# u*B of 16 of the 64 tiles made with time on the partitions, in a 12-layer state-space kernel

## The chip, the cores and the metric

The kernel runs on one core of one Trainium2 chip. The metric is the device time in microseconds; three runs gave 21105.7 to 21121.04 us, median 21120.72.

## The reference

The input x has 8 images of 256 channels and 32x32 = 1024 points; the points are the time steps. Twelve layers follow each other. A layer does, for each image (einsums written short):

```
xn = layernorm(x); xp = xn @ proj_w + pb; z = silu(xp)
forward:  xs = softplus(xp @ convf_w + b);   backward: the same with convb_w, time reversed
delta, B, C = split(xs @ dbc_w)      # 32 ranks, 16 states of B, 16 states of C
delta = softplus(delta @ dtp_w + dtp_b)
h[t] = exp(delta[t]*A[n]) * h[t-1] + (delta[t]*xs[t]) * B[t,n]     # per channel and state n
y[t] = sum over n of h[t]*C[t,n];    y += xs*D
out = x + (y_forward + y_backward) * z
```

With u = delta*xs, the input of the scan of state n is u[channel, t] * B[t, n]. All data are float32.

## The kernel before

An image in a layer is one iteration; there are 12 x 8 = 96 of them. Channels stand on the 128 partitions (two channel halves), time runs along the free dimension (1024 columns). One iteration has 64 tiles: channel half (k // 32), direction ((k // 16) % 2), state (k % 16). In one tile:

- ScalarE makes dA = exp(delta * A[n]) (`tile_exp`, L507) into one of four buffers.
- TensorE replicates row n of B over all partitions into PSUM (`rep_b`, L666, two bf16 matmuls: B is held as three bf16 parts and `select` adds them), VectorE multiplies it by u in place (`times_b`, L802), and scans (`scan`, L818) into a ring of eight buffers.
- A DMA on SyncE loads row n of C, broadcast over the partitions (`load_c`, L285), GpSimd multiplies the scan by it (`product`, L356), and TensorE adds the result into y by a matmul with the identity (`add_up`, L676), five tiles later (LAG).

Eight of the 64 tiles (`SHARED`) do without TensorE and VectorE's multiply: SyncE loads the row of B from HBM (L291), GpSimd multiplies it by u into `v` (L364), and ScalarE puts exp into the PSUM buffer that B would have had.

Each engine has its own instruction list and goes through it in order. The list is written as slots, one per tile. VectorE takes two tiles at a time: multiply k, multiply k+1, scan k, scan k+1. TensorE's slot k is: `rep_b` of tile k+2 (it waits for scan k, which frees the PSUM buffer), the add-up of tile k-5, any `add_skip` (xs*D by a diagonal matrix, L687), then `prepare(k)`. `prepare` is the work for the next iteration (layernorm, projections, softplus, B and C, delta and u): tables such as `CONV_AT`, `DTP_AT` say in which slot each step stands, with first and second entries for the two directions, and for halves or channel groups. ScalarE's tables count three slots later (`AHEAD`): its `prepare(k)` comes after the exp of tile k+3. TensorE's preparation matmuls are L694 (over two channel halves, 4 instructions) and L741 (one matmul, 2 instructions), through two PSUM banks `bank[0]`, `bank[1]`, which ScalarE empties: `both_signs` (L511 Abs and L512 Relu) after projections and after L741. GpSimd's are the normalisation (L372), the sums of softplus (L391, L396), the split of B into bf16 parts (L381, L386) and u (L404). VectorE has the centring (L832) and the gate `finish` (L824), which waits for the last add-up of a channel half. The waits are semaphores: `h_ready` counts scans, `p_ready` products, `summed` add-ups, `b_ready` replications, `u_ready` u's, `dtp_out` emptied banks.

Of the kernel before, what the change touches and what calls it, by code (L numbers as in the profile page):

```python
# [17 lines left out]
def conv_seq_kernel(nc, x, ln_g, ln_b, proj_w, proj_b, convf_w, convf_b, convb_w, convb_b,  # L18
# [17 lines left out]
    NDA, NR, NC = 4, 8, 4  # L36
# [845 lines left out]
```

## Time and profile before

| | busy us | share of the span |
|---|---|---|
| VectorE (DVE) | 20038.9 | 95% |
| GpSimd (POOL) | 19962.6 | 95% |
| TensorE (PE) | 18408.8 | 87% |
| ScalarE (ACT) | 11624.8 | 55% |
| DMA read from HBM | 3744.62 MB | 184 GB/s over the span |
| span of the profiled execution | 21097.6 | |
| its own device time | 21099.31 | |
| median of the three runs | 21120.72 | |

The busy time of an engine is the time in which one of its instructions was running; two that overlap count once. A row of the timeline has the start, the length of a run of equal instructions, and in brackets the idle time before it and what ended it. The granted clock of TensorE was 0.979 of full speed on the average.

### The profile page before, as it was taken

To read this page: it belongs to the slowest core of one execution; us is meant where nothing else is said; L and a number is where in the kernel's file an instruction comes from. 1 tells how busy PE (TensorE), PEld (TensorE's weight loads), DVE (VectorE), ACT (ScalarE), POOL (GpSimd) and SP (SyncE) were. 2 spreads that over 40 slices of the span, in tenths; PEclk is the share of its full clock that TensorE was granted. 3 is DMA by queue.
4 is the path that set the end of the run, shared out by engine and by line. 5 is a ranking of instruction groups with operands and counts; after the bars stand their busy time and mean duration, and the time that the engine had idled before them with its cause. 6 is when DMAs were issued, how large, how long until landed. Compare 5 with 4: busy or idle time off the path is not lost.

```text
span 21097.6 us, 191673 instructions
## 1 busy us (share of the span) xinstructions
PE 18408.8 (87%) x45506; PEld 7540.0 (36%) x46368; DVE 20038.9 (95%) x11904; ACT 11624.8 (55%) x12409; POOL 19962.6 (95%) x8174
## 2 busy tenths in 40 slices
PE   8888888888888888888888888888888888888888
PEld 3333333333333333333333333333333333333333
DVE  7999999999999999999999999999999999999999
ACT  5555555555555555555555555555555555555554
POOL 8999999999999999999999999999999999999998
PEclk9999999999999999999999999999999999999999
DMA  5555555555555555555555555555555555555555
GB/s 170 184 186 185 187 179 190 183 184 186 181 186 186 183 187 183 188 181 186 185 186 186 181 189 183 185 186 182 187 184 182 187 184 188 181 186 186 184 186 175
DMA packets 1101818, 3886.20 MB, mean 184 GB/s; under 512 B 147584, under 2 KB 158336, under 8 KB 1100416
## 3 DMA queue, kind: packets, MB, share of 16 engines
q1 hardware_dynamic: 1023616, 3733.38, 50.5%
q0 software_dynamic: 26112, 100.67, 2.7%
q10 hardware_dynamic: 50688, 36.88, 0.7%
q8 instruction: 463, 7.59, 0.1%
q14 instruction: 939, 7.69, 0.1%
HBM read 3744.62 MB, written 134.22 MB: 184 GB/s over the span
## 4 chain that ended last, share of the span: by engine, by line
issue 34%; DVE 20%; PE 19%; POOL 17%; ACT 4%; DMA 4%; DVEq 1%; ACTq 1%; POOLq 0%; SPq 0%
DVE ring L818 13%; PE y L676 11%; POOL ring L356 10%; DVE bv L802 6%; DMA c<-c_rows 4%; PE bv L666 3%; PE bank L694 3%; POOL delta L396 3%; ACT dA L507 2%; POOL parts L386 1%; PE bank L741 1%; DVE w L832 1%; POOL u L404 1%; POOL v L364 1%; POOL dbc L381 1%
## 5 line engine op out<-in xcount | busy, mean ns | idle before, releaser
L356 POOL TENSOR_TENSOR ring<-ring,c 128x1024 f32<-128x1024 f32 x6144 | 14327.9, 2372 | 209.8 <-DVE ring L818 200.8
L676 PE MATMUL y<-ring,ident 128*128 128x512 f32 x24576 | 11798.1, 608 | 620.3 <-POOL ring L356 526.8
L818 DVE TENSOR_TENSOR_SCAN ring<-dA,bv 128x1024 f32<-128x1024 f32 x5376 | 12021.6, 2271 | 100.2
L507 ACT ACTIVATE dA<-delta,a_step 128x1024 f32<-128x1024 f32 x5376 | 6022.4, 1146 | 2834.1 <-DVE ring L818 2238.9
L802 DVE TENSOR_TENSOR bv<-u,bv 128x1024 f32<-128x1024 f32 x5376 | 6332.4, 1214 | 844.7 <-POOL u L404 416.8
L676 PEld LDWEIGHTS y<-ring,ident 128*128 128x128 f32 x24576 | 4759.9, 195 | 4967.1 <-issue 3536.8
L666 PE MATMUL bv<-parts,select 128*128 128x512 bf16 x9890 | 3111.5, 390 | 1915.7 <-DVE ring L818 1856.0
L666 PEld LDWEIGHTS bv<-parts,select 128*128 128x128 bf16 x10752 | 729.5, 99 | 5732.1 <-DVE ring L818 5122.7
L507 ACT ACTIVATE bv<-delta,a_step 128x1024 f32<-128x1024 f32 x768 | 859.5, 1119 | 2426.8 <-DVE ring L818 2289.4
L364 POOL TENSOR_TENSOR v<-u,v 128x1024 f32<-128x1024 f32 x768 | 1812.3, 2360 | 124.6 <-DMA v<-c_rows 123.3
L818 DVE TENSOR_TENSOR_SCAN ring<-bv,v 128x1024 f32<-128x1024 f32 x768 | 1739.3, 2265 | 24.3 <-ACT bv L507 24.1
L694 PE MATMUL bank<-z,wt 128*128 128x512 f32 x3072 | 1442.5, 592 | 0.8 <-ACT z L533 0.8
L511 ACT ACTIVATE tmp<-bank,vec 128x512 f32<-128x512 f32 x768 | 525.4, 684 | 1155.3 <-PE bank L694 927.4
L372 POOL TENSOR_TENSOR w<-w,tmp 128x1024 f32<-128x1024 f32 x192 | 453.9, 2364 | 725.5 <-ACT tmp L608 725.5
L511 ACT ACTIVATE pre<-bank,vec 128x512 f32<-128x512 f32 x768 | 527.5, 687 | 924.2 <-PE bank L694 571.8
L741 PE MATMUL bank<-dbc,wt_dbc 128*128 128x512 f32 x1536 | 777.4, 608 | 119.5 <-ACT delta L512 113.7
L694 PEld LDWEIGHTS bank<-z,wt 128*128 128x128 f32 x3072 | 583.5, 190 | 735.9 <-issue 731.9
L694 PE MATMUL bank<-pre,mean_w 128*128 128x512 f32 x1536 | 733.3, 600 | 6.5 <-DMA pre<-in_x_dram 5.8
L694 PE MATMUL bank<-w,wt 128*128 128x512 f32 x1536 | 692.8, 594 | 1.3 <-ACT wt L492 1.3
L527 ACT ACTIVATE pre<-w 128x1024 f32<-128x1024 f32 x192 | 202.9, 1057 | 772.0 <-DVE w L832 772.0
L559 ACT COPY dbc<-bank 128x512 f32<-128x512 f32 x384 | 220.3, 574 | 636.5 <-POOL parts L386 397.4
L533 ACT ACTIVATE z<-bank,pbias 128x512 f32<-128x512 f32 x384 | 251.6, 680 | 524.4 <-PE bank L694 524.4
(65 smaller groups left out, 10686.0 us busy)
## 6 DMA issues: line engine op xcount, KB each, us to landing
c<-c_rows SPq DMA_DIRECT2D x6144, 512.0 KB, 4.5
v<-c_rows SPq DMA_DIRECT2D x768, 512.0 KB, 5.0
out_dram<-z POOLq DMA_DIRECT2D x96, 1024.0 KB, 11.9
pre<-out_dram SPq DMA_DIRECT2D x88, 1024.0 KB, 5.2
c_rows<-dbc ACTq DMA_DIRECT2D x192, 128.0 KB, 1.9
pre<-in_x_dram SPq DMA_DIRECT2D x8, 1024.0 KB, 5.0
out_dram<-in_x_dram SPq DMA_DIRECT2D x8, 1024.0 KB, 15.9
raw_w<-in_L_conv_proj_w_dram ACTq DMA_DIRECT2D x12, 256.0 KB, 5.3
```

The lines of the kernel that those rows point to most:

```text
L356: nc.gpsimd.tensor_tensor(ring[k % NR][:], ring[k % NR][:], c_sb[k % NC][:], ALU.mult).then_inc(p_ready, 1)
L364: nc.gpsimd.tensor_tensor(v_sb[:], u_of(d, s)[:, c, :], v_sb[:], ALU.mult).then_inc(vp_ready, 1)
L372: nc.gpsimd.tensor_tensor(wh, wh, tmp[:, 0:1, half(h)].to_broadcast([P, DT, HALF]), ALU.mult).then_inc(normed, 1)
L396: nc.gpsimd.tensor_tensor(delta_of(d, s)[:], delta_of(d, s)[:], scratch[j][:], ALU.add).then_inc(delta_ready, 1)
L507: nc.scalar.activation(to[:], delta_of(d, s)[:, c, :], ACT.Exp, scale=a_step[s][:, c, n:n + 1]).then_inc(da_ready, 1)
L511: nc.scalar.activation(scratch[j][:, e, half(h)], bank[i % 2][:], ACT.Abs, bias=bias).then_inc(abs_done, 1)
L666: mm = pe.matmul(bv[k % 2][:, half(h)], select[:, n:n + 1].to_broadcast([P, P]), parts_of(d, s)[:, half(h)], start=True, stop=True)
L676: mm = pe.matmul(y[:, half(h)], ident[:], ring[k % NR][:, half(h)], start=(k % HALF_TILES == 0), stop=(k % HALF_TILES == HALF_TILES - 1), ...
L694: mm = pe.matmul(dst[:], lhs(c), rhs[:, c, half(h)], start=(c == 0), stop=(c == DT - 1))
L741: pe.matmul(bank[i % 2][:], wt_dbc[:, DT + e, :], dbc[:, half(h)], start=True, stop=True).then_inc(dtp_ready, 1)
L802: nc.vector.tensor_tensor(bv[k % 2][:], u_of(d, s)[:, c, :], bv[k % 2][:], ALU.mult).then_inc(v_ready, 1)
L818: nc.vector.tensor_tensor_scan(h, a, b, 0.0, ALU.mult, ALU.add).then_inc(h_ready, 1)
```

## The change

No tile is shared with GpSimd any more. For 16 tiles (`BY_T`: every odd tile from 17 to 31 and from 49 to 63) u*B is made as follows.

- B of the direction of these tiles is turned once per iteration: TensorE transposes the eight 128-column blocks of `dbc` (`turn_b`), ScalarE copies the 16 columns of each block out (`b_t`, time on the partitions).
- u of the channel half and direction of these tiles is turned twice per iteration, for tiles 16 to 31 and for 48 to 63: TensorE transposes eight blocks into the two banks (`turn_u`), ScalarE copies them to `u_t`. In the next slot with preparation work TensorE waits for these copies.
- For each of the 16 tiles ScalarE scales the eight blocks of `u_t` by the column of `b_t` (one value of B per time step, that is per partition) into `v_t` (`scale_u`), right after the exp of the tile before, and TensorE transposes the eight blocks back into the PSUM buffer `bv` (`turn_v`), where `rep_b` of the tile would stand. VectorE scans from there, with dA from SBUF.

The loads of B rows on SyncE and the products u*B on GpSimd are gone. There are three dA buffers instead of four (tile 63 takes the buffer of 61). HELD goes from 2 to -21. The tables of `prepare`, `SKIPS`, `LOADX_AT` (50 to 63) and `W_AT` are new. At the very end GpSimd's memset writes `mark`.

```diff
-    NDA, NR, NC = 4, 8, 4
-    SHARED = (9, 19, 23, 29, 35, 45, 55, 59)
-    B_AHEAD, V_AHEAD = 5, 6
-    LAG, HELD = 5, 2
+    NDA, NR, NC = 3, 8, 4
+    BY_T = (17, 19, 21, 23, 25, 27, 29, 31, 49, 51, 53, 55, 57, 59, 61, 63)
+    UT_GROUPS = (1, 3)
+    UT_AT, UT_OUT_AT = (1, 37), (1, 36)
+    BLOCKS = T // P
+    LAG, HELD = 5, -21
...
-    MEAN_AT, CENTRE_AT, SQUARE_AT = (3, 4), (8, 10), (7, 10)
-    VAR_AT, RSTD_AT, NORM_AT = (9, 11), (11, 15), (9, 16)
-    PROJ_AT, XP_AT = (15, 15, 19, 19), (16, 16, 19, 19)
-    CONV_AT = ((22, 23, 25, 27), (29, 31, 33, 35))
-    CONV_OUT_AT = ((21, 23, 28, 29), (29, 30, 33, 34))
-    XS_LOG_AT, XS_AT = ((31, 32), (35, 35)), (35, 39)
-    DBC_AT, DBC_OUT_AT = ((37, 39), (47, 49)), ((37, 39), (47, 48))
-    DTP_AT, DTP_OUT_AT = ((41, 41, 41, 42), (49, 51, 51, 51)), ((40, 41, 42, 42), (50, 50, 52, 52))
-    HI_AT, REST_AT, MID_AT, PARTS_AT = (40, 49), (44, 53), (45, 57), (47, 55)
-    DELTA_LOG_AT, DELTA_AT, U_AT = ((43, 47), (55, 55)), (47, 55), (47, 57)
-    DIAG_AT, A_STEP_AT = 49, 53
-    GATE_AT = 37
-    LOADX_AT = 50
-    W_AT = 55
-    SKIPS = ((13, 9), (51, 55))
+    MEAN_AT, CENTRE_AT, SQUARE_AT = (3, 7), (6, 9), (7, 9)
+    VAR_AT, RSTD_AT, NORM_AT = (9, 11), (11, 11), (10, 15)
+    PROJ_AT, XP_AT = (13, 17, 18, 18), (18, 18, 20, 21)
+    CONV_AT = ((23, 23, 26, 26), (31, 31, 33, 35))
+    CONV_OUT_AT = ((23, 23, 26, 29), (31, 32, 32, 35))
+    XS_LOG_AT, XS_AT = ((30, 31), (35, 36)), (36, 38)
+    DBC_AT, DBC_OUT_AT = ((37, 38), (43, 48)), ((37, 37), (46, 50))
+    BT_AT, BT_OUT_AT = 39, 38
+    DTP_AT, DTP_OUT_AT = ((39, 40, 40, 41), (50, 51, 51, 51)), ((40, 40, 40, 41), (50, 51, 52, 52))
+    HI_AT, REST_AT, MID_AT, PARTS_AT = (38, 50), (42, 55), (43, 55), (44, 56)
+    DELTA_LOG_AT, DELTA_AT, U_AT = ((42, 44), (52, 56)), (46, 56), (47, 57)
+    DIAG_AT, A_STEP_AT = 47, 31
+    GATE_AT = 40
+    LOADX_AT = 63
+    W_AT = 54
+    SKIPS = ((13, 9), (51, 56))
...
+        def da_of(k):
+            return k % NDA if k < TILES - 1 else (k - 2) % NDA
+        def da_gap(k):
+            return next(g for g in range(1, 2 * NDA) if da_of((k - g) % TILES) == da_of(k))
...
 # ScalarE
-                if k in SHARED:
-                    act.wait_ge(h_ready, tiles(it, k - 1))
-                    to = bv[k % 2]
-                else:
-                    act.wait_ge(h_ready, tiles(it, k + 1 - NDA))
-                    to = dA[k % NDA]
+                act.wait_ge(h_ready, tiles(it, k + 1 - da_gap(k)))
...
+            def turn_u(it, g):
+                for h in range(NH):
+                    act.wait_ge(ut_turned, uts(it, g) + (h + 1))
+                    act.wait_ge(vt_ready, others(it, g * NS))
+                    nc.scalar.copy(u_t[:, h * (BLOCKS // NH):(h + 1) * (BLOCKS // NH), :].rearrange("p b d -> p (b d)"),
+                                   bank[h][:]).then_inc(ut_out, 1)
+            def scale_u(it, k, s):
+                n, g = k % NS, k // NS
+                act.wait_ge(ut_out, uts(it, g) + NH)
+                act.wait_ge(bt_out, it * NH + NH)
+                act.wait_ge(v_turned, others(it, k))
+                for q in range(BLOCKS):
+                    one = nc.scalar.activation(v_t[:, q, :], u_t[:, q, :], ACT.Copy, scale=b_t[s][:, q, n:n + 1])
+                one.then_inc(vt_ready, 1)
...
 # TensorE
+            def turn_b(n, j):
+                pe.wait_ge(dbc_out, n * 4 + 2 * j + 2)
+                for q in range(BLOCKS):
+                    h, r = q // (BLOCKS // NH), q % (BLOCKS // NH)
+                    mm = pe.transpose(bank[h][:, r * P:(r + 1) * P], dbc[:, q * P:(q + 1) * P], ident[:])
+                mm.then_inc(bt_turned, 1)
...
+            def turn_v(it, k):
+                pe.wait_ge(vt_ready, others(it, k + 1))
+                pe.wait_ge(h_ready, tiles(it, k - 1))
+                for q in range(BLOCKS):
+                    mm = pe.transpose(bv[k % 2][:, q * P:(q + 1) * P], v_t[:, q, :], ident[:])
+                mm.then_inc(v_turned, 1)
...
                         if k == DTP_AT[j][i]:
+                            if j == 0 and i == 0:
+                                pe.wait_ge(bt_out, n * NH + NH)
...
-                    if (k + 2) % TILES in SHARED:
-                        pass
+                    if (k + 2) % TILES in BY_T:
+                        turn_v(it, k + 2)
...
+                    for g, at in zip(UT_GROUPS, UT_AT):
+                        if k == at:
+                            turn_u(it, g, at, s, more)
+                        if k == next(f for f in range(at, TILES) if f in fills) and more:
+                            pe.wait_ge(ut_out, uts(it, g) + NH)
...
 # VectorE
-                if k in SHARED:
-                    dve.wait_ge(vp_ready, others(it, k + 1))
-                    a, b = bv[k % 2][:], v_sb[:]
+                if k in BY_T:
+                    dve.wait_ge(v_turned, others(it, k + 1))
```

## Rows read from the trace of the kernel before

**Rows 1.** The page, part 1: busy us (share of the span) x instructions.
```profile
PE 18408.8 (87%) x45506; PEld 7540.0 (36%) x46368; DVE 20038.9 (95%) x11904; ACT 11624.8 (55%) x12409; POOL 19962.6 (95%) x8174
```

**Rows 2.** Groups of instructions by form: xcount | busy us, mean ns | idle before, releasers.
```profile
L356 POOL TENSOR_TENSOR ring<-ring,c 128x1024 f32<-128x1024 f32 x6144 | 14327.9, 2372 | 209.8 <-DVE ring L818 200.8 <-issue 4.7 <-DMA c<-c_rows 1.5
L818 DVE TENSOR_TENSOR_SCAN ring<-dA,bv 128x1024 f32<-128x1024 f32 x5376 | 12021.6, 2271 | 100.2
...
L802 DVE TENSOR_TENSOR bv<-u,bv 128x1024 f32<-128x1024 f32 x5376 | 6332.4, 1214 | 844.7 <-POOL u L404 416.8 <-PE bv L666 339.6 <-issue 88.2
...
L364 POOL TENSOR_TENSOR v<-u,v 128x1024 f32<-128x1024 f32 x768 | 1812.3, 2360 | 124.6 <-DMA v<-c_rows 123.3
```

**Rows 3.** Timeline of VectorE, a shared and an own pair: start us, us, instruction.
```profile
10001.73 1.21 DVE L802 TENSOR_TENSOR bv<-u,bv 128x1024 f32<-128x1024 f32 x1
10003.07 2.29 DVE L818 TENSOR_TENSOR_SCAN ring<-dA,bv 128x1024 f32<-128x1024 f32 x1
...
10007.45 2.33 DVE L802 TENSOR_TENSOR bv<-u,bv 128x1024 f32<-128x1024 f32 x2
10009.70 4.46 DVE L818 TENSOR_TENSOR_SCAN ring<-dA,bv 128x1024 f32<-128x1024 f32 x2
10014.07 1.21 DVE L802 TENSOR_TENSOR bv<-u,bv 128x1024 f32<-128x1024 f32 x1
```

**Rows 4.** The gate's line, 9900 to 10900 us: ns min/median/max, first and last start.
```profile
L824 DVE TENSOR_TENSOR z<-y,z x9: 1225/1225/1225, 9959.5 to 10836.3; 128x1024 f32<-128x1024 f32 x9
```

**Rows 5.** Waits over the span: us in total, times, longest us.
```profile
DVE bv L802 <- POOL u L404: 416.8, 96, 91.5
...
DVE bv L802 <- PE bv L666: 339.6, 274, 1.8
```

**Rows 6.** Timeline of GpSimd at the end of an iteration.
```profile
10151.58 4.50 POOL L404 TENSOR_TENSOR u<-delta,xf 128x2048 f32<-128x2048 f32 x1
```

**Rows 7.** The page, part 6: KB each, median us from issue to landing.
```profile
pre<-out_dram SPq DMA_DIRECT2D x88, 1024.0 KB, 5.2
```

**Rows 8.** Timeline of TensorE, slots of around tile 50.
```profile
10323.99 0.61 PE L666 MATMUL bv<-parts,select 128*128 128x512 bf16 x2
10324.44 1.88 PE L676 MATMUL y<-ring,ident 128*128 128x512 f32 x4
10326.15 1.88 PE L694 MATMUL bank<-xf,wt_dbc 128*128 128x512 f32 x4
10327.87 1.02 PE L741 MATMUL bank<-dbc,wt_dbc 128*128 128x512 f32 x2
```

**Rows 9.** Transposes of weights, timeline; then a stretch: us, busy, PEclk, DMA, GB/s.
```profile
19098.19 0.38 PE L644 MATMUL bank<-ident,raw_dbc 128*128 128x128 f32 x2
19098.41 0.38 PE L644 MATMUL bank<-ident,raw_dtp 128*128 128x128 f32 x2
19098.63 1.88 PE L676 MATMUL y<-ring,ident 128*128 128x512 f32 x4
...
19097.00:19100.00 3.00, 0.60 (x4) 0.50 (x4) 1.00 1.00 391
```

**Rows 10.** Timeline of ScalarE: column scalings, exp, Abs, Relu.
```profile
10330.54 0.69 ACT L599 ACTIVATE diag_d<-ident,vec 128x128 f32<-128x128 f32 x2
10331.13 1.14 ACT L507 ACTIVATE dA<-delta,a_step 128x1024 f32<-128x1024 f32 x1
10332.17 0.67 ACT L511 ACTIVATE tmp<-bank,vec 128x512 f32<-128x512 f32 x1
10332.74 0.68 ACT L512 ACTIVATE delta<-bank,vec 128x512 f32<-128x512 f32 x1
```

**Rows 11.** Timeline of VectorE: the multiply of tile 25 waits for TensorE.
```profile
10240.07 1.23 DVE L802 TENSOR_TENSOR bv<-u,bv 128x1024 f32<-128x1024 f32 x1 [1.26 <-PE bv L666]
```

**Rows 12.** TensorE's last L741 of slot 51, and VectorE behind it.
```profile
10337.21 1.10 PE L741 MATMUL bank<-dbc,wt_dbc 128*128 128x512 f32 x2 [0.59 <-ACT delta L512]
...
10338.77 1.23 DVE L802 TENSOR_TENSOR bv<-u,bv 128x1024 f32<-128x1024 f32 x1 [1.61 <-PE bv L666]
```

More of the change, by code:

```diff
@@ L123, in conv_seq_kernel @@
         c_sb = [sb(f"c{i}", [P, T]) for i in range(NC)]
-        v_sb = sb("v", [P, T])
+        u_t = sb("u_t", [P, BLOCKS, P])
+        v_t = sb("v_t", [P, BLOCKS, P])
+        b_t = [sb(f"b_t{s}", [P, BLOCKS, NS]) for s in range(2)]
         raw_w = sb("raw_w", [P, DT, D])
@@ L141, in conv_seq_kernel @@
         eps = sb("eps", [P, 1])
+        mark = sb("mark", [P, 1])
         c_rows = nc.dram_tensor("c_rows", (2, DIRS, BC, T), F32, kind="Internal").ap()
@@ L425, in tail @@
                 pool.wait_ge(gated, it * DT + DT)
-                nc.gpsimd.memset(v_sb[:, 0:1], 0.0)
+                nc.gpsimd.memset(mark[:], 0.0)
                 finish(it, s, b)
@@ L559, in prepare @@
                             nc.scalar.copy(dbc[:, half(h)], bank[h][:]).then_inc(dbc_out, 1)
+                    if j == 0 and k == BT_OUT_AT:
+                        act.wait_ge(bt_turned, n + 1)
+                        for h in range(NH):
+                            nc.scalar.copy(b_t[s][:, h * (BLOCKS // NH):(h + 1) * (BLOCKS // NH), :],
+                                           bank[h][:].rearrange("p (b r) -> p b r", r=P)[:, :, 0:NS]).then_inc(bt_out, 1)
                     for i, (e, h) in enumerate(layers_steps):
@@ L613, in slots @@
                     tile_exp(it, k, s)
+                    if k + 1 in BY_T:
+                        scale_u(it, k + 1, s)
+                    for g, at in zip(UT_GROUPS, UT_OUT_AT):
+                        if k - AHEAD == at:
+                            turn_u(it, g)
                     if more:
@@ L668, in rep_b, with banks_free, turn_u @@
                 mm.then_inc(b_ready, 1)
+            def turn_b(n, j):
[4 more added lines that the diff above has]
+                mm.then_inc(bt_turned, 1)
+            def banks_free(k, n):
+                if k <= MEAN_AT[0]:
+                    pe.wait_ge(dtp_out, n * (2 * FILLS))
+                elif PROJ_AT[-1] < k <= CONV_AT[0][0]:
+                    pe.wait_ge(xp_ready, n * FILLS + FILLS)
+                elif CONV_AT[0][-1] < k <= CONV_AT[1][0]:
+                    pe.wait_ge(conv_out, n * (2 * FILLS) + FILLS)
+                else:
+                    assert CONV_AT[1][-1] < k <= DBC_AT[0][0]
+                    pe.wait_ge(conv_out, n * (2 * FILLS) + 2 * FILLS)
+            def turn_u(it, g, at, s, more):
+                c, d = g // DIRS, g % DIRS
+                if g == UT_GROUPS[0]:
+                    pe.wait_ge(u_ready, it * 2 + 2)
+                else:
+                    pe.wait_ge(ut_out, uts(it, g))
+                if more:
+                    banks_free(at, it + 1)
+                for q in range(BLOCKS):
+                    h, r = q // (BLOCKS // NH), q % (BLOCKS // NH)
+                    mm = pe.transpose(bank[h][:, r * P:(r + 1) * P], u_of(d, s)[:, c, q * P:(q + 1) * P], ident[:])
+                    if r == BLOCKS // NH - 1:
+                        mm.then_inc(ut_turned, 1)
+            def turn_v(it, k):
+                pe.wait_ge(vt_ready, others(it, k + 1))
+                pe.wait_ge(h_ready, tiles(it, k - 1))
+                for q in range(BLOCKS):
+                    mm = pe.transpose(bv[k % 2][:, q * P:(q + 1) * P], v_t[:, q, :], ident[:])
+                mm.then_inc(v_turned, 1)
             def add_up(it, k):
@@ L838, in slots @@
                     times_b(it, k, s)
-                    if k + 1 not in SHARED:
+                    if k + 1 not in BY_T:
                         times_b(it, k + 1, s)
```

39 lines of the change are left out of this document (18 added, 21 removed).

## The prediction

> **What bounds the kernel now.** I read the busy shares first. VectorE and GpSimd are both busy 95% of the span, TensorE 87%, ScalarE 55% [rows 1]. The costliest groups say what the two do: for each of 6144 tiles GpSimd makes one product by C (2.33 us apart), and for 768 of them it also makes u*B (2.36 us); VectorE makes one scan per tile (2.2 us apart) and 5376 products u*B [rows 2]. The timeline of VectorE gives the true step costs. A pair of tiles that VectorE prepares itself takes 6.62 us (10007.45 to 10014.07). A pair with one shared tile takes 5.72 us (10001.73 to 10007.45): two back-to-back products cost 1.12 each, but a lone one costs 1.34, because the scan waits for its result [rows 3]. So a tile taken away from VectorE is worth 0.90 us, not the 1.21 of its product.
>
> The gate operations show the period: nine of them, two per iteration (one image through one layer), from 9959.5 to 10836.3, so 876.8/4 = 219.2 us [rows 4]. VectorE's work in it: 24 pairs x 6.62 + 8 x 5.72 = 204.6, and two gates and two centrings of 1.1 to 1.2 with 0.3 of wait at each gate, about 5.1 together: 209.7. The rest, 9.5 us, is waiting. The waits name it: 416.8 us for GpSimd's u (91.5 of it the prologue, so 3.4 per iteration) and 339.6 for TensorE's B (3.5 per iteration) [rows 5]. The first is GpSimd's own load: it starts the last u at 10151.58 and ends it after 10156.0, when the next iteration could have begun [rows 6].
>
> **What the change takes away.** Turned tiles go from 8 (shared) to 16. VectorE: eight more pairs become 5.72: -8 x 0.90 = -7.2 us, 202.5 left. GpSimd loses 8 products, 8 x 2.36 = -18.9 of its 19962.6/96 = 207.9 us, 189 left: it is no bound any more, and its waits for the B rows go. The last u is then ready before VectorE asks: with its queue in order (rest, parts, delta and u come to 13 us, u alone 4.5, beside products of 2.33) I get the end of u about 0.7 us ahead. So I take the wait of 3.4 as gone, and what is late next is TensorE and ScalarE. SyncE loses 8 loads of 512 KB; its load of the next image moves from slot 50 to 63. The only cover is the four slots (some 12 us) to the mean at slot 3, against 5.2 us to landing [rows 7]; were it later, TensorE would stand there with B of the next tiles queued behind.
>
> **What it adds on TensorE.** In its stream a replication of B takes 0.45 us, an add-up of a tile 1.71, a projection over two channel halves 1.72, a single one 0.86 [rows 8]. Before: 64 x 1.71 + 56 x 0.45 + 56 single projections x 0.86 = 183 us. Four transposes of 128x128 take 0.44 us between their neighbours (19098.19 to 19098.63), 0.11 each, at granted clock 1.00 [rows 9]. So a turned tile costs 8 x 0.11 = 0.88 instead of no replication; u twice and B once are 24 more. Added 152 x 0.11 = 16.7, taken away 8 x 0.45 = 3.6: 196 us of work beside VectorE's 202.5.
>
> The Trainium skill ("TensorE: Matmul & The Clock Gate", Part 4: PE-mode transpose) speaks against this: it gives about 275 ns per transpose in a kernel and says that transposes do not count as activity for the clock. By 275 ns, 152 would be 42 us and TensorE's sum 221 us, above the present period. The rows have two transposes in 0.38 us, so 0.27 for one alone and 0.11 for each next one; a turn is eight in a row, and I go by the 0.11.
>
> **What it adds on ScalarE.** Two scalings of 128x128 by a column, the same form as the new ones, take 0.59 us before the next starts: 0.295 each; an exponential 1.04; an Abs or Relu out of PSUM 0.57 [rows 10]. A turned tile costs 8 x 0.295 = 2.36, 16 of them 37.8 per iteration. With four 512-column copies of u (0.57) and two small ones of B (64 columns, not in the trace: above 0, below the 0.295 of 128 columns, I take 0.25) that is 11624.8/96 = 121 + 41 = 162 us. On the average that is hidden. It is not in places, since ScalarE is in order: behind a wait stand the exponentials for VectorE.
>
> **Edits at nothing.** Three dA buffers instead of four make an exponential wait for the scan three tiles before; its cover is ScalarE's idle time (the exponential still has two scans, 4.4 us, for 1.04 of work), and it is gone only in tiles 49 to 59, counted below. The hold of the add-ups never acted: a tile is due five slots later, past either threshold. The mark memset is one small instruction at the end. Prologue: some 10 transposes and small copies, 1 to 3 us once.
>
> **Where the waits come, slot by slot.** A slot on TensorE is: B for tile k+2 (or the turn of k+2), the add-up of k-5, then its preparation work. It begins when scan k is done. VectorE needs B(k+2) 1.1 to 3.3 us later. One projection in an even slot of pairs that VectorE makes itself costs 0.45 + 1.71 + 1.72 + 0.6 = 4.5 against 3.2, a stall of 1.3; the trace has it: 1.26 at 10240.07 [rows 11]. I replay the new tables by these numbers.
> - Slots 15 to 31 (turned pairs): TensorE needs 8 x (0.45 + 0.88) + 16 x 1.71 = 38.0 and 7 projections x 1.72 = 12.0, sum 50; VectorE wants 45.8. Two projections in slot 18 make the turn of 21 late by 1.95; two in slot 23 make B of 26 late by 1.3; two in 26 the turn of 29 by 1.5; two in slot 31 B of 35 by 1.1. Together 5.8, of which 4.2 is plain excess of work.
> - Slots 36 to 41: slot 37 waits for ScalarE's copies of u, the projection of slot 38 then makes B of 41 late by 1.4. Slot 39 waits for B turned and copied out, slot 40 for the third single projection until ScalarE has emptied a bank, and B of 43 is late by 2.3. Together 3.7.
> - Slots 47 to 62: ScalarE has, for tiles 49 to 59, 11 x 1.04 + 5 x 2.36 + about 11.9 of preparation (eight Abs or Relu of 0.57; by their lengths at 1.04 per 1024 columns two copies of 512, two casts of 1024, two passes of 2048; the diagonal's two scalings) = 35 us; VectorE wants 31.5, and ScalarE's lead is 2 to 4.5. The sharp place is slot 51: TensorE's last single projection waits for an output that ScalarE gives only after exp 54 and the scaling for 55, and behind it stands B of 54: late by 3.7. The kernel before has this wait too, at 1.61 [rows 12]; there no scaling of 2.36 is in front.
> The sum of stalls is 13.3. The remaining places (slots 0 to 14) I take at zero, as fills stand in odd slots.
>
> **The sum.** 202.5 + 13.3 = 215.8 us per iteration against 219.2, -3.4 x 96 = -326 us. The profiled execution took 21099.3 (span 21097.6); the median is 21.4 above it. 21099.3 - 326 + 21.4 = 20795; I say 20800, 1.5% faster. The bounds of the stalls: no more than before without the u wait (9.5 - 3.4 = 6.1) gives 208.6, 20100 us, which leaves no place for the 4.2 of plain excess in slots 15 to 31 beside the rest; the full excess with serial scalings is the second rival.
>
> **Rivals.**
> 1. The stalls overlap, since a stall in one place gives TensorE and ScalarE time in the next, and only the 9.5 of before remain: 202.5 + 9.5 = 212.0, -7.2 x 96 = -691: 20430. For it: the single stalls before are short (largest 1.61 in the stretch), and a replay takes every latency as fixed. Against: in slots 15 to 31 the work alone is over by 4.2. Chance 0.22.
> 2. No change. Stalls of 16.7 eat all: TensorE at 196 us with its waits has too little room. For it: it is now within 7 us of VectorE. Time 21120. Chance 0.08.
> 3. Slower: ScalarE sets the pace of turned tiles. The place is the scaling before each turn; the price is 0.10 us per instruction if scalings follow at their own length (0.69 - 0.295 = 0.395) instead of overlapping, 0.8 per tile. It is on the path in the five tiles of 49 to 59 (4.0) and in about half of the other turned tiles' slots where TensorE has no slack (some 2.4): 222.2, +3.0 x 96: 21410. It decides from 0.34 us per tile in ten tiles on (3.4 us). Against: the pair in the rows does overlap. Chance 0.13.
> 4. Transposes lower TensorE's clock or are not streamed. A turn of 2.2 us instead of 0.88 adds 1.3 x 16 = 21 us to an engine with 6.5 of room: 215.8 + 14.5 = 230, over 22100. Against: [rows 9]. The rule of the skill above is this rival. Chance 0.02.
>
> My forecast (20550 to 21000) has 0.55. A measurement of this kernel can tell about 0.2%, 42 us, from no change. Faster 0.77, same 0.08, slower 0.15. The range 20400 to 21110 takes in rival 1 and the case of no change nearly whole.
>
> **What would show it.** Right: the costliest groups have 4608 products u*B on VectorE, pairs with a turned tile 5.72 apart where nothing waits, GpSimd busy near 18200 us, ScalarE near 15500; the wait for u falls to the prologue's; the waits for the turned tiles and for B add to 13 us per iteration, the largest in slots 51 to 54. Wrong: a turn that takes over 1 us on TensorE, a period over 219, a granted clock below the present one in slots 15 to 31 or 47 to 62, GpSimd's u still late, or scans that wait for dA outside tiles 49 to 59.

## The result, and the profile after

The changed kernel takes 21302.45 us (median of 4 runs, 21285.25 to 21323.57) against 21116.17 us before in the same session: ratio 1.009 [1.0077, 1.0102]. It is 0.9% slower. I had forecast 20800, 1.5% faster, and the range ended at 21110. The profiled execution took 21309.66 us (span 21308.0, +210.4 against the span before); the mean granted clock is 0.988, against 0.979 before.

The page after, part 1, answers to [rows 1]; then the costliest groups by form, to [rows 2] (xcount | busy us, mean ns | idle before, releasers).

```profile
PE 19440.8 (91%) x59424; PEld 8999.9 (42%) x59424; DVE 19301.3 (91%) x11136; ACT 15481.2 (73%) x25273; POOL 18274.1 (86%) x7406
```

```profile
L372 POOL TENSOR_TENSOR ring<-ring,c 128x1024 f32<-128x1024 f32 x6144 | 14369.7, 2364 | 2709.1 <-DVE ring L898 2627.0 <-issue 41.7 <-DMA c<-c_rows 39.4
L898 DVE TENSOR_TENSOR_SCAN ring<-dA,bv 128x1024 f32<-128x1024 f32 x6144 | 13730.7, 2273 | 576.7 <-PE bv L739 326.1 <-ACT dA L511 45.1 <-PE y L748 2.4
...
L883 DVE TENSOR_TENSOR bv<-u,bv 128x1024 f32<-128x1024 f32 x4608 | 5491.6, 1215 | 1340.0 <-PE bv L697 1163.5 <-POOL u L414 90.3 <-issue 85.8
...
L527 ACT ACTIVATE v_t<-u_t,b_t 128x128 f32<-128x128 f32 x12288 | 3756.0, 396 | 664.9 <-PE bv L739 654.9
...
L739 PE MATMUL bv<-ident,v_t 128*128 128x128 f32 x12288 | 1616.3, 275 | 65.3 <-ACT v_t L527 61.1 <-DVE ring L898 3.4
```

VectorE has 4608 products left and 737.6 us less of work. GpSimd now idles 2709 us, nearly all for VectorE's scans, so on the average it is no bound. ScalarE's 15481 and GpSimd's 18274 are the forecast sizes. And VectorE's waits (answer to [rows 5]; us in total, times, longest):

```profile
DVE bv L883 <- PE bv L697: 1163.5, 553, 5.2
DVE ring L898 <- PE bv L739: 326.1, 201, 2.0
DVE bv L883 <- POOL u L414: 90.3, 1, 90.3
DVE bv L883 <- issue: 85.8, 34, 4.2
...
DVE ring L898 <- ACT dA L511: 45.1, 31, 4.2
```

The wait for u fell from 416.8 to the prologue's 90.3, as forecast. The wait for B rose from 339.6 to 1163.5, and 326.1 for turned tiles came in. So: 737.6 of work and 326.5 of wait for u gone, 823.9 + 326.1 of waits for TensorE come; the other 124 or so of the +210 are small. About 100 are the 0.13 us by which a scan waits for a lone product, in eight more pairs per iteration (the prediction's 0.90 per tile has them), and 21 are waits for ScalarE's exponentials (45.1 after, 24.1 before).

The period, over the whole run, is (21296.4 - 231.3)/95.5 = 220.58 us. Before it is (21086.3 - 229.2)/95.5 = 218.40, not the 219.2 that I read from four periods [rows 4]. The gate's line after, then before (first and last start):

```profile
L904 DVE TENSOR_TENSOR z<-y,z x192: 1224/1225/1226, 231.3 to 21296.4; 128x1024 f32<-128x1024 f32 x192
```

```profile
L824 DVE TENSOR_TENSOR z<-y,z x192: 1223/1225/1226, 229.2 to 21086.3; 128x1024 f32<-128x1024 f32 x192
```

With VectorE's floors of the prediction (209.7 and 202.5) the kernel before loses 8.7 us per iteration, the new one 18.1. The change is worth something as long as the loss stays below 218.4 - 202.5 = 15.9. That is the number to hold every experiment against.

By tile, VectorE's waits after are (mean us of the waits in some 95 iterations, worked out from its timeline):

| tile that waits | 21 | 26 | 29 | 35 | 41 | 43 | 54 | sum |
|---|---|---|---|---|---|---|---|---|
| forecast | 1.95 | 1.3 | 1.5 | 1.1 | 1.4 | 2.3 | 3.7 | 13.3 |
| measured | 1.86 | 1.34 | 1.39 | 0.92 | 2.37 | 2.08 | 4.65 | 14.6 |

All seven places are where the replay put them. Behind the largest stands this. TensorE around slot 51 (start us, us, instruction, [idle before it <- what ended it]), then ScalarE beside it, then VectorE:

```profile
10220.15 0.59 PE L697 MATMUL bv<-parts,select 128*128 128x512 bf16 x2
10220.58 1.88 PE L748 MATMUL y<-ring,ident 128*128 128x512 f32 x4
10222.30 1.02 PE L817 MATMUL bank<-dbc,wt_dbc 128*128 128x512 f32 x2
10223.16 1.04 PE L739 MATMUL bv<-ident,v_t 128*128 128x128 f32 x8
10224.03 1.88 PE L748 MATMUL y<-ring,ident 128*128 128x512 f32 x4
10225.75 1.88 PE L759 MATMUL y<-xf,diag_d 128*128 128x512 f32 x4
10227.47 1.88 PE L817 MATMUL bank<-dbc,wt_dbc 128*128 128x512 f32 x4
10230.23 1.10 PE L817 MATMUL bank<-dbc,wt_dbc 128*128 128x512 f32 x2 [0.88 <-ACT delta L532]
10231.16 0.59 PE L697 MATMUL bv<-parts,select 128*128 128x512 bf16 x2
```

```profile
10225.45 1.16 ACT L511 ACTIVATE dA<-delta,a_step 128x1024 f32<-128x1024 f32 x1
10226.50 2.44 ACT L527 ACTIVATE v_t<-u_t,b_t 128x128 f32<-128x128 f32 x8
10228.84 0.67 ACT L531 ACTIVATE tmp<-bank,vec 128x512 f32<-128x512 f32 x1
10229.41 0.68 ACT L532 ACTIVATE delta<-bank,vec 128x512 f32<-128x512 f32 x1
```

```profile
10231.79 1.23 DVE L883 TENSOR_TENSOR bv<-u,bv 128x1024 f32<-128x1024 f32 x1 [4.55 <-PE bv L697]
```

I had said that TensorE waits for an output that stands behind ScalarE's scaling of 55. ScalarE's order is as I said (exp, eight scalings, Abs, Relu), but TensorE waits only 0.88 us for it. It is late before: it turns 53 at 10223.16, 1.6 us after scan 51 ended (10217.06 + 4.46 for the pair of scans 50 and 51), and then has 7.07 us (10223.16 to 10230.23, the wait included) ahead of the last single projection. B of 54 is late mostly by TensorE's work; the runs below test that.

### The profile page after: what moved, and what is told of

It reads as the page before. It is cut to its first block, busy times and chain, and to the rows that moved or that the text cites. A ratio compares the mean times of both kernels' runs of the same rounds, so it can differ in the third digit from the quotient of the medians.

```text
span 21308.0 us, 234433 instructions
## 1 busy us (share of the span) xinstructions
PE 19440.8 (91%) x59424; PEld 8999.9 (42%) x59424; DVE 19301.3 (91%) x11136; ACT 15481.2 (73%) x25273; POOL 18274.1 (86%) x7406
## 4 chain that ended last, share of the span: by engine, by line
PE 43%; issue 25%; DVE 15%; ACT 11%; POOL 4%; ACTq 1%; DVEq 1%; DMA 0%; POOLq 0%
PE y L748 23%; PE bank L766 10%; DVE ring L898 9%; DVE bv L883 5%; PE bv L697 5%; ACT v_t L527 4%; ACT dA L511 4%; PE bv L739 4%; POOL ring L372 3%; ACT delta L532 1%; PE y L759 1%; PE bank L817 1%; ACT tmp L539 1%; DVE w L912 1%; ACT tmp L531 1%
## 5 line engine op out<-in xcount | busy, mean ns | idle before, releaser
L898 DVE TENSOR_TENSOR_SCAN ring<-dA,bv 128x1024 f32<-128x1024 f32 x6144 | 13730.7, 2273 | 576.7 <-PE bv L739 326.1
L511 ACT ACTIVATE dA<-delta,a_step 128x1024 f32<-128x1024 f32 x6144 | 6936.4, 1147 | 3038.5 <-DVE ring L898 2886.3
L883 DVE TENSOR_TENSOR bv<-u,bv 128x1024 f32<-128x1024 f32 x4608 | 5491.6, 1215 | 1340.0 <-PE bv L697 1163.5
L527 ACT ACTIVATE v_t<-u_t,b_t 128x128 f32<-128x128 f32 x12288 | 3756.0, 396 | 664.9 <-PE bv L739 654.9
L697 PE MATMUL bv<-parts,select 128*128 128x512 bf16 x9216 | 2805.8, 387 | 1342.6 <-DVE ring L898 1324.2
L739 PEld LDWEIGHTS bv<-ident,v_t 128*128 128x128 f32 x12288 | 1421.5, 141 | 945.0 <-issue 749.4
L739 PE MATMUL bv<-ident,v_t 128*128 128x128 f32 x12288 | 1616.3, 275 | 65.3 <-ACT v_t L527 61.1
L518 ACT COPY u_t<-bank 128x512 f32<-128x512 f32 x384 | 206.3, 589 | 474.8 <-PE bank L731 474.8
L532 ACT ACTIVATE delta<-bank,vec 128x512 f32<-128x512 f32 x768 | 525.0, 684 | 0.0
L817 PEld LDWEIGHTS bank<-dbc,wt_dbc 128*128 128x128 f32 x1536 | 267.7, 189 | 549.9 <-issue 482.6
```

The lines of the kernel that those rows point to most:

```text
L511: nc.scalar.activation(dA[da_of(k)][:], delta_of(d, s)[:, c, :], ACT.Exp, scale=a_step[s][:, c, n:n + 1]).then_inc(da_ready, 1)
L527: one = nc.scalar.activation(v_t[:, q, :], u_t[:, q, :], ACT.Copy, scale=b_t[s][:, q, n:n + 1])
L532: nc.scalar.activation(to[:, e, half(h)], bank[i % 2][:], ACT.Relu, bias=bias).then_inc(done, 1)
L697: mm = pe.matmul(bv[k % 2][:, half(h)], select[:, n:n + 1].to_broadcast([P, P]), parts_of(d, s)[:, half(h)], start=True, stop=True)
L739: mm = pe.transpose(bv[k % 2][:, q * P:(q + 1) * P], v_t[:, q, :], ident[:])
L817: pe.matmul(bank[i % 2][:], wt_dbc[:, DT + e, :], dbc[:, half(h)], start=True, stop=True).then_inc(dtp_ready, 1)
```

## Experiments

Each was timed beside the kernel before; the mean of VectorE's waits by tile comes from its timeline. Ratios are to the kernel before.

### Whose time are the waits: TensorE's turns or ScalarE's scalings?

e1 leaves out seven of the eight transposes of a turned tile, e2 seven of its eight scalings. What they compute is no longer the scan's input; they are there for their time.

```diff
 # e1, turn_v
-                for q in range(BLOCKS):
+                for q in range(1):
                     mm = pe.transpose(bv[k % 2][:, q * P:(q + 1) * P], v_t[:, q, :], ident[:])
 # e2, scale_u
-                for q in range(BLOCKS):
+                for q in range(1):
                     one = nc.scalar.activation(v_t[:, q, :], u_t[:, q, :], ACT.Copy, ...)
```

> Leaves out 7 of the 8 transposes with which TensorE turns u*B of a tile back into PSUM (the values scanned there are stale), so that TensorE has 16 x 7 x 0.109 = 12.2 us less per iteration and everything else, waits included, stays. Theory A (the lost time is TensorE's order of work: it is over its room in slots 15 to 31, and its waits put B of 54, 41, 43 late): the waits at tiles 21, 26, 29, 35 (5.5 us per iteration) shrink to at most 1.5, those at 41, 43, 54 stay within 0.9, about -4 us per iteration, 20920 us. Rival B (ScalarE's 8 scalings per turned tile set the pace): within 1 us per iteration of the changed kernel, 21200 to 21310. Rival C (no engine's work matters, the time goes at loop ends and layer ends): no change in the waits at 21 to 35, 21300.

Measured: 20771.64 us, 0.9838 [0.9822, 0.9855]; 531 us less than the changed kernel. The waits at 21, 26 and 29 fall to 0.29, 0.29 and 0.24, at 35 to 0.69, at 54 to 3.81; 41 and 43 stay (2.38, 2.08). Seven transposes fewer in 16 tiles are 7 x 0.11 x 16 = 12.3 us of TensorE, and VectorE gets 5.6 of them back (period 215.0). Theory A had said 4, 20920 us.

> Leaves out 7 of the 8 scalings per turned tile on ScalarE (the other blocks are zero from a memset at the start): 33 us less per iteration on ScalarE; TensorE's transposes stay. Theory A: only the wait of tile 54 feels it, 4.65 minus 7 x 0.295 = 2.6 us, and the waits at layer ends (scans 59 to 61) go; -2.3 us per iteration, 21080. Rival B (ScalarE sets the pace): -5 us or more per iteration, under 20830. Rival C: under 0.5 us per iteration.

Measured: 21277.9 us, 1.0077 [1.006, 1.0094]; 24 us less than the changed kernel, which the two intervals do not tell apart. 54 still waits 4.48, the others do not move: theory A's 2.6 us at 54 did not come, and the number is that of rival C. 112 scalings per iteration, 33 us of ScalarE, are worth 0.3 us. So in this order the waits are TensorE's work; the scalings, my rival 3 among others, are not on the path. What they do once TensorE has less to do, e5 shows.

### The order at slot 51

```diff
 # e3: at tile 54 ScalarE's preparation ahead of the scaling of 55
-                    if k + 1 in BY_T:
+                    if k + 1 in BY_T and k not in (54,):
                         scale_u(it, k + 1, s)
...
                         prepare(k - AHEAD, it + 1, 1 - s)
+                    if k in (54,):
+                        scale_u(it, k + 1, s)
 # e5: the add-ups of xs*D (4 matmuls each) from slots 51 and 56 to 47 and 61
-    SKIPS = ((13, 9), (51, 56))
+    SKIPS = ((13, 9), (47, 61))
```

> One call moved: at tile 54 ScalarE empties the bank that TensorE's last single projection of slot 51 waits for (and its other preparation) before it scales for tile 55, not after. Nothing is left out. Theory A (it is the order on ScalarE that puts B of 54 late): the wait at 54 falls from 4.65 by the 2.36 of the scaling to 2.3, none takes its place, -2.3 x 95 = -220 us, 21080. Rival D (TensorE has no room left, 196 of 202 us, so a wait that goes comes back at the next tiles): waits of 55 to 63 grow by about 2, the time stays over 21230.

Measured: 21603.61 us, 1.0231 [1.0214, 1.0248], 301 slower than the changed kernel. The wait at 54 falls by 0.3 only, not by the 2.36 of theory A: ScalarE now waits for TensorE before it can give the output, so with the scaling out of the way TensorE's own work keeps B of 54 at 4.3 late. The scaling of 55 stands behind outputs that ScalarE itself waits for, that of 57 behind them too, the turn of 57 comes late, and new waits stand at 57, 58 and 59. ScalarE at tile 54, then TensorE at the turn of 57, and its clock behind the wait (columns as under e5):

```profile
10151.35 0.69 ACT L531 ACTIVATE tmp<-bank,vec 128x512 f32<-128x512 f32 x1 [1.92 <-PE bank L819]
```

```profile
10158.44 0.59 PE L699 MATMUL bv<-parts,select 128*128 128x512 bf16 x2
10158.87 1.88 PE L750 MATMUL y<-ring,ident 128*128 128x512 f32 x4
10163.58 1.96 PE L741 MATMUL bv<-ident,v_t 128*128 128x128 f32 x8 [2.83 <-ACT v_t L527]
10165.34 2.42 PE L750 MATMUL y<-ring,ident 128*128 128x512 f32 x4
```

```profile
10163.00:10165.00 2.00, 1.42 (x7) 1.43 (x8) 0.70 (x1) 2.00 (x4) 2.00 (x2) 0.50 0.67 201
```

After 2.83 us without work, eight transposes take 1.96 us instead of 1.04 and an add-up 2.42 instead of 1.88: the granted clock is 0.50, the 1.2 GHz level. This happens in 70 of the 95 iterations, not in all.

> Two add-ups of xs*D (1.72 us each on TensorE) are moved from slots 51 and 56 to 47 and 61. Nothing is left out. In the changed kernel's trace TensorE enters slot 51 already 1.5 us late and does 7.0 us of work there, then waits 0.9 for ScalarE's output. Theory A2 (two limits in one place: TensorE's work, and 0.9 us behind it ScalarE's chain exp 54, scaling 55, output): with 1.72 less work TensorE only waits 2.6 instead of 0.9 for ScalarE, the wait at 54 stays at 4.5 to 4.65, 21290 us. Rival E (TensorE's work alone puts B of 54 late): the wait falls by 1.7 to 2.9, -1.7 us per iteration, 21140.

Measured: 21571.92 us, 1.0221 [1.0204, 1.0238], 269 slower than the changed kernel. With 1.72 us of work taken out of slot 51, TensorE waits for ScalarE instead, 2.60 where it was 0.88 (as theory A2 had it), but 54 waits 5.90, not 4.5 to 4.65. That is 1.2 of the 2.7 us per iteration lost; the rest stands where the two add-ups went, at tiles 50 and 51 (1.0 together) and 1 (0.5). TensorE, and its busy time and granted clock in stretches (us, PE busy, PEld, DVE, ACT, POOL, PEclk, DMA share, GB/s):

```profile
10128.71 1.88 PE L817 MATMUL bank<-dbc,wt_dbc 128*128 128x512 f32 x4
10133.19 1.43 PE L817 MATMUL bank<-dbc,wt_dbc 128*128 128x512 f32 x2 [2.60 <-ACT delta L532]
10134.42 1.06 PE L697 MATMUL bv<-parts,select 128*128 128x512 bf16 x2
10135.27 2.86 PE L748 MATMUL y<-ring,ident 128*128 128x512 f32 x4
```

```profile
10126.00:10130.00 4.00, 4.00 (x16) 2.21 (x15) 3.60 (x2) 3.68 (x6) 4.00 (x3) 1.00 0.49 176
10130.00:10133.00 3.00, 0.59 (x2) 0.00 (x0) 0.00 (x0) 3.00 (x10) 3.00 (x2) 1.00 0.72 244
10133.00:10135.00 2.00, 1.81 (x4) 0.70 (x5) 0.00 (x0) 2.00 (x4) 2.00 (x2) 0.71 0.65 203
10135.00:10139.00 4.00, 4.00 (x15) 2.33 (x14) 3.35 (x2) 4.00 (x5) 2.96 (x2) 0.72 0.62 223
```

The granted clock is 1.00 until the wait and 0.71 and 0.72 behind it, the mean of a part at 1.2 and a part at 2.4 GHz: the pair for B takes 1.06 us, not 0.59, and the add-up 2.86, not 1.88. In the changed kernel the same stretch stays at 1.00:

```profile
10223.00:10228.00 5.00, 5.00 (x19) 2.69 (x18) 4.25 (x2) 4.64 (x10) 5.00 (x3) 1.00 0.54 158
10228.00:10232.00 4.00, 3.12 (x9) 1.15 (x8) 0.21 (x1) 4.00 (x9) 4.00 (x3) 1.00 0.68 229
```

The clock does not fall each time, though the wait is 2.60 in all 95 iterations. In 36 of them the last projection keeps its length and 54 waits 5.15; in 59 it is longer and 54 waits 6.35. So some 0.5 of the rise at 54 is the order (ScalarE's exp of 54 and all behind it start later against the scans, since the turn of 51 is late) and 0.7 is the clock.

TensorE and ScalarE come to 54 within 2 us of each other, and taking either's work away leaves the other: the scalings gone (e2) or moved (e3), TensorE's work leaves 4.5 and 4.3; TensorE's add-up gone, ScalarE's output leaves 5.2 and more. The Trainium skill ("TensorE: Matmul & The Clock Gate", Part 1: HAM oscillation) has the same pattern, a wait that leaves the clock at half for the next burst; its waits are 3 to 5 us, and the rows here show it already behind 2.60.

### The turn of u one step later

```diff
 # e4
-    UT_AT, UT_OUT_AT = (1, 37), (1, 36)
+    UT_AT, UT_OUT_AT = (1, 42), (1, 42)
```

(`banks_free` gets a branch for slot 42: the outputs of the first direction.)

> The second turning of u (for tiles 48 to 63) is moved from slot 37, where TensorE waits for ScalarE's two copies before its first projection, to slot 42, between the last single projection and the next direction's. Nothing is left out. Theory A: the wait of about 4 us inside slot 37 goes, so B of 41 is late by the 1.26 of one projection in an even slot instead of 2.37, B of 43 by at most 2.1: -1.1 to -2.5 us per iteration, 21060 to 21200. Rival D: the 0.9 us of transposes and the wait for the copies reappear as a wait at tiles 44 to 47, no gain, 21300.

Measured: 21598.09 us, 1.0229 [1.0212, 1.0246], 296 slower. 41 waits 2.00 instead of 2.37, 43 as before 2.09, and a new wait of 3.06 stands at 45, as in rival D but larger. TensorE in e4:

```profile
10309.51 1.98 PE L768 MATMUL bank<-w,wt_dbc 128*128 128x512 f32 x4 [1.34 <-POOL w L402]
...
10332.44 1.06 PE L733 MATMUL bank<-ident,u 128*128 128x128 f32 x8 [2.02 <-ACT delta L532]
```

At slot 42 the turn waits 2.02 us for an output that ScalarE gives only after its work on the gate, and then takes its own 0.9 us. Nor is the turn what makes 41 late: without it the projection of slot 37 waits for GpSimd's sum `w`. The changed kernel has in the same place, TensorE and then GpSimd:

```profile
10172.42 1.96 PE L748 MATMUL y<-ring,ident 128*128 128x512 f32 x4 [1.02 <-DVE z L904]
10174.21 1.04 PE L731 MATMUL bank<-ident,u 128*128 128x128 f32 x8
10176.12 1.98 PE L766 MATMUL bank<-w,wt_dbc 128*128 128x512 f32 x4 [0.88 <-ACT u_t L518]
```

```profile
10171.05 4.54 POOL L402 TENSOR_TENSOR w<-w,pre 128x2048 f32<-128x2048 f32 x1
```

The add-up of the slot first waits 1.02 us for VectorE's gate. I had started the replay behind it, at 1.4, and 1.4 + 1.02 is the measured 2.4. The equality does not show that the gate is the limit: GpSimd ends `w` at 10175.59, 0.5 us before the projection starts, so with an earlier gate, or without the turn, the projection could start at most those 0.5 us earlier.

### Spreading TensorE's work

If TensorE's order is the cause, an order with the projections in odd slots and further apart must bring VectorE's time back, with the same instructions. e6 changes the order of slots 34 to 61, e7 that of slots 3 to 35, e8 both. The diff shows TensorE's steps; the entries for ScalarE and GpSimd (outputs, norm, logarithms, the split of B, the gate of z) follow them by one to three slots, and in e8 B is turned in slot 41, not 39.

```diff
 # e6 (back) and e8
-    DBC_AT, DBC_OUT_AT = ((37, 38), (43, 48)), ((37, 37), (46, 50))
+    DBC_AT, DBC_OUT_AT = ((37, 39), (45, 47)), ((37, 39), (47, 47))    # e6: 38 and 37 for the first 39s
-    DTP_AT, ... = ((39, 40, 40, 41), (50, 51, 51, 51)), ((40, 40, 40, 41), (50, 51, 52, 52))
+    DTP_AT, ... = ((41, 41, 43, 43), (49, 49, 51, 51)), ((42, 42, 43, 43), (49, 49, 51, 51))  # e6: first parts as they were
-    SKIPS = ((13, 9), (51, 56))
+    SKIPS = ((11, 7), (47, 61))                                        # e6: (13, 9); e7: (51, 56)
 # e7 (front) and e8
-    MEAN_AT, CENTRE_AT, SQUARE_AT = (3, 7), (6, 9), (7, 9)
+    MEAN_AT, CENTRE_AT, SQUARE_AT = (3, 5), (4, 6), (5, 7)
-    PROJ_AT, XP_AT = (13, 17, 18, 18), (18, 18, 20, 21)
+    PROJ_AT, XP_AT = (11, 13, 13, 15), (11, 13, 14, 15)
-    CONV_AT = ((23, 23, 26, 26), (31, 31, 33, 35))
+    CONV_AT = ((17, 21, 25, 29), (31, 33, 33, 35))
-    LOADX_AT = 63
+    LOADX_AT = 52
...
```

> The preparation of slots 43 to 56 is laid out anew: the projections of slots 43, 48 go to 45, 47, the four single ones of slots 50, 51, 51, 51 to 49, 49, 51, 51, their outputs on ScalarE to 49, 49, 51, 51 (so the last one no longer waits for an output made two tiles later), the two add-ups of xs*D to 47 and 61, one ln pass from 56 to 54. The same instructions in all. Theory A2: TensorE has at most one slot of 5.2 us, both limits are moved, the wait at 54 (4.65) falls under 0.7: -4 us per iteration, 20920 us. Rival D (no room left on TensorE or ScalarE in tiles 49 to 63): waits for v or dA of 3 us or more appear at 55 to 63; 21250.

Measured: 21333.2 us, 1.0108 [1.0091, 1.0125], +31, which is not clear of noise; the forecast of 20920 missed. Rival D's 21250 is nearer, though its single waits of 3 us or more did not come. 54 falls from 4.65 to 0.63, but 50, 52, 57, 58 and 59 now wait 0.6 to 1.3 each: that stretch has no room left, only places.

> The preparation of slots 3 to 29 is laid out anew: mean, variance, normalisation and the first projections two to four slots earlier (slots 3 to 15, all odd), the four projections of the first direction one each in slots 17, 21, 25, 29 instead of two in 23 and two in 26; the load of the next image back at slot 52. The same instructions in all; in slots 16 to 31 TensorE has 4 projections instead of 7. Theory A2 (local excess of work on TensorE, which has idle time in slots 0 to 14): the waits at 21, 26, 29 (1.86, 1.34, 1.39) go, 35 stays: -4.5 us per iteration, 20880. Rival D: what is packed into slots 3 to 15 makes waits there of the same size; 21250 to 21300.

Measured: 21103.51 us, 0.9996 [0.9986, 1.0005], 199 less than the changed kernel. 21, 26 and 29 are gone (-4.6), and of 35 0.36 is left at 33; 15, 18, 20 and 37 wait 0.6 to 0.7 each. The period falls by 2.2, half of the forecast 4.5.

> Both of the layouts of the two runs before, and slots 37 to 43 as well: one projection each in 37 and 39, B turned and two single projections in 41, the other two in 43 (before: 38, 39, 40, 40, 41), the gate's silu from 40 to 38. The same instructions in all. Theory A2: the waits at 41, 43, 54, 21, 26, 29 go but for some 1 to 2 us in all: -11 to -13 us per iteration, 20050 to 20250, faster than the kernel before by 4 to 5%. Rival D: TensorE's 196 us and ScalarE's 162 leave no more than half of it: 20600 to 20900.

Measured: **20832.82 us (20823.87 to 20834.6), 0.9867 [0.9851, 0.9884]**: 1.3% faster than the kernel before and 470 us under the changed one, with the same scans, products, scalings and turns. That is rival D's number (20600 to 20900), not theory A2's (20050 to 20250): the order gives back 5.0 us per iteration where I had said 11 to 13. e7 alone has 2.2 of them and e6 none, so some 2.9 should be due to slots 37 to 43, which no run has alone; there 41 falls to 0.66, 43 is gone, and 45 waits 0.53. VectorE's waits:

```profile
DVE bv L883 <- PE bv L697: 772.6, 1152, 1.6
DVE ring L898 <- ACT dA L511: 143.5, 74, 7.4
...
DVE ring L898 <- PE bv L739: 68.0, 102, 1.4
```

1152 waits of 0.67 us on the average in place of 553 of 2.1 us. Many short waits are dearer than they look. In VectorE's timeline an own pair takes 6.62 us without a wait and 6.72 beside the wait with one in it (325 pairs of the changed kernel), a turned pair 5.72 and 5.83 (192 pairs): the instructions overlap by 0.1 us, and a wait takes that away. At 4.4 waits per iteration before, 8.5 in the changed kernel and 14.2 in e8 (gates left out) this makes about 0.4, 0.9 and 1.4 us.

### Is it the order or the turned tiles?

e9 is the kernel before with the order of e8. e10 is e8 with tiles 17 to 31 turned only, e11 is e8 with none turned and none shared.

```diff
 # e10, e11 against e8
-    BY_T = (17, 19, 21, 23, 25, 27, 29, 31, 49, 51, 53, 55, 57, 59, 61, 63)
+    BY_T = (17, 19, 21, 23, 25, 27, 29, 31)      # e11: ()
-    UT_GROUPS = (1, 3)
+    UT_GROUPS = (1,)                             # e11: ()
```

> The kernel before (8 tiles shared with GpSimd, nothing turned) with the order of preparation steps of the spread version. It tells how much of the 20832.8 us of that version is the order and how much the turned tiles. Theory T (the turned tiles pay once the order lets them): here GpSimd stays at 207.9 us of work per iteration and its wait for u (3.4 per iteration) stays; only part of the other 5.3 us of waits can go, so between 21110 and 20800, I say 20950, and GpSimd's u is still the largest wait of VectorE. Theory O (the order alone made the gain, the turn nothing): 20830 or below, with waits at tiles 3, 25 and 54 gone and u in time.

> The spread version with only tiles 17 to 31 turned (8 of 64); those of 49 to 63 are made by VectorE. By theory T each turned tile is worth 0.90 us of VectorE less what it brings in waits; the eight tiles of 49 to 63 then cost 8 x 0.90 = 7.2 less their waits (50, 52, 54, 57 and the dA of 59 in the spread version, about 4 per iteration together): +3.2 x 96, 21140. ScalarE's wait at 59 goes (its 18.9 us of scalings in that stretch are gone). If the turned tiles of 49 to 63 bring nothing (theory O) it is at 20830 or below; if their waits are not their own, up to 21500.

> The spread version with no tile turned and none shared: VectorE makes all 64 products u*B. Floor of VectorE 32 x 6.62 + 5.1 = 216.9 us per iteration. Theory T: floor plus some 3 us of waits, 219.9 against the 215.6 of the spread version, 21250 (range 21100 to 21450). Theory O (order alone): 20830 or below, which the floor excludes unless pairs run under 6.62. It also gives the loss of an order without turns: if the sum of waits is as large as in the spread version, the waits left there are not due to the turns.

| kernel | us | ratio | period | VectorE's floor | loss |
|---|---|---|---|---|---|
| e11, none turned | 21849.71 | 1.0356 [1.0338, 1.0373] | 226.1 | 216.9 | 9.2 |
| e10, 17 to 31 | 21119.34 | 1.0008 [0.9998, 1.0017] | 218.5 | 209.7 | 8.8 |
| e8, all 16 | 20832.82 | 0.9867 [0.9851, 0.9884] | 215.6 | 202.5 | 13.1 |
| e9, before's tiles | 21772.74 | 1.0316 [1.0299, 1.0334] | 225.4 | 209.7 | 15.7 |

The periods are those of the gates. In one order, the eight turned tiles 17 to 31 are worth 7.6 us, 0.95 each (0.90 forecast); the eight of 49 to 63 only 2.9, 0.37 each, since their work brings 4.3 us of waits. With eight turned tiles (e10) the kernel is as fast as with the eight shared ones before. Theory O (the order made the gain alone) falls: with this order and no turned tiles the kernel is slower than before. My 21140 for e10 holds; for e11 I was 600 us too low, and outside my range, because I took 3 us of loss, and this order loses about 9 with no turned tile as with eight. So waits of that size come with the preparation in this order, and not with the turns. Not tested is the other half: sixteen turned tiles in the order of the kernel before.

For e9 I had said 20950, with GpSimd's u as the largest wait; it took 820 us more, and u is in time. It loses for a reason of its own, at tile 59. VectorE's waits, then VectorE, ScalarE and GpSimd in one iteration (each with its own start times):

```profile
DVE ring L818 <- ACT bv L507: 672.9, 104, 8.5
DVE bv L802 <- PE bv L666: 595.8, 776, 2.0
DVE bv L802 <- POOL u L404: 91.5, 1, 91.5
```

```profile
10244.28 2.29 DVE L818 TENSOR_TENSOR_SCAN ring<-bv,v 128x1024 f32<-128x1024 f32 x1 [6.47 <-ACT bv L507]
...
10242.10 1.04 ACT L580 CAST parts<-dbc 64x1024 bf16<-64x1024 f32 x1 [12.27 <-POOL dbc L381]
10243.05 1.11 ACT L507 ACTIVATE bv<-delta,a_step 128x1024 f32<-128x1024 f32 x1
...
10239.96 2.11 POOL L381 TENSOR_TENSOR dbc<-dbc,parts 96x1024 f32<-96x1024 f32 x1
```

The scan of 59 waits for ScalarE's exp, but ScalarE is not late by its own work: it stands 12.27 us at a cast that needs GpSimd's split of B, and GpSimd, which here has the eight shared products as well, comes to the split only at 10239.96. Over the run ScalarE waits 1154.4 us for it. The order of e8 has this cast two slots earlier than the kernel before (55, not 57) and the split two slots later (55, not 53), which fits a GpSimd with 18.9 us less to do. So e9 does not measure the order alone. The wait is 6.48 us at tile 59 in nearly every iteration; taken off, the period would be 219.0, still no gain. GpSimd's work is the same as before (19948.8 us, 19962.6 before); that its u is in time here is probably because VectorE needs 225.4 us.

## Why the prediction was wrong

- **What was removed: right.** 0.90 us per tile (0.95 in the tiles where nothing else came), GpSimd at 18274 us for a forecast near 18200, the wait for u down to the prologue's.
- **What was added: right.** TensorE's eight transposes take 0.87 us to the next instruction (0.88 forecast), at granted clock 1.00. TensorE's busy time per iteration rose by 10.7 us (202.5 after, 191.8 before, from the pages) for a forecast of 13.1; my 183 and 196 are both too low against it, since the profile's busy time has more than my steps. In one of the shortest iterations, 10062.45 to 10280.67, it is 199.87. Eight scalings take 2.34 to 2.36 to the next instruction (2.36 forecast); ScalarE's 15481 us were forecast near 15500. The Trainium skill's rule ("TensorE: Matmul & The Clock Gate", Part 4: PE-mode transpose) is not borne out as a price: the mean length of one is its 275 ns, but eight in a row take 0.87 us, and the clock stays. Rival 4 is out.
- **The step that failed is the stall sum of 13.3 us**, in "Where the waits come, slot by slot". Its period of 215.8 was 220.6. Of the 4.8: the seven places measured 14.6, +1.2 per iteration (41 left out the wait for the gate, and 54 TensorE's own lateness); "the remaining places I take at zero" left out what the kernel before also has, its loss of 8.7 less the named 3.4, 1.6 and 1.25, so 2.45 us (VectorE's own issue 0.92, tile 3 0.44, layer ends 0.5, the rest small gaps); and about 1.1 came new, half of it dA and turned tiles at layer starts and ends, and 0.4 the 0.10 us that each of some four more waits costs VectorE beside its length. The base was 0.8 too high besides: four periods gave 219.2, all 95 give 218.4. With both corrected and nothing else, 202.5 + 13.3 + 2.45 = 218.25 against 218.4 is no change, and the break-even loss of 15.9 was 0.15 away. The sign hung on terms that I had set to zero.
- **The mechanism at 54 was half right.** Place and order were; of the cause named, the scaling ahead of the output, the trace shows 0.88 us of wait in 4.55, and with seven of eight scalings gone (e2) 4.48 of 4.65 stay, with the scaling moved behind the output (e3) 4.3.
- **Rivals.** Rival 1 (stalls overlap) was wrong in the changed kernel, but its loss of 9.5 is near what e10 reaches in a better order (8.8). Rival 3 had the sign, with a false mechanism: without seven eighths of the scalings the kernel is 24 us faster at most (e2). Rival 2 was the nearest, with a chance of 0.08: stalls of 16.7 because TensorE has too little room; the loss was 18.1. The slower outcome I should have priced is the plain one that goes on from there: TensorE at 91% of the span with double projections in one slot. The edits that the prediction put at nothing were not tested one by one: the trace has 21 us more of waits for exponentials with three dA buffers than with four, and no run changes the hold of the add-ups alone.

## What to carry to other kernels

A forecast made of a floor and a sum of stalls needs the same sum for the kernel before, down to its measured loss, and a break-even loss next to it: what stays unexplained there is a term of the kernel after too. Where work is moved to an engine that is nearly full, the order of its single steps decides the sign: the same instructions took 21302 and 20833 us. Where two engines arrive at a place together, taking work from one gives nothing, or less than nothing. And the engine that ends a wait is not yet its cause: ask what that engine itself waited for (e9, tile 59).

## What the runs showed of the hardware

- After waits of 2.60 (e5) and about 2.8 us (e3) in a TensorE that is otherwise busy, the next matmuls were slower in 59 and 70 of 95 iterations; in those shown the granted clock was 0.71 and 0.50 over the next 2 us (pair for B 1.06 us, not 0.59; add-up 2.86, not 1.88). After 0.88, in the changed kernel, they kept their length in all 95. Work taken out ahead of a wait can thus make what stands behind it later.
- The transposes in the stream did not lower the clock: 0.988 for the run with 14592 of them, 0.979 before. The iteration from 10062.45 to 10280.67 has 1.00.
- A change of 33 us per iteration on ScalarE (73% busy) moved the time by 24 us of 21302, within the noise; 12.3 us per iteration on TensorE (91% busy) moved it by 531.
- A wait costs VectorE 0.10 us beside its length: a pair of 6.62 us takes 6.72 besides the wait.
